# LN1's per-token scale and shift worked out once for eight attention units, the v copies split around the exponential, and a mask moved ahead of a projection

## The reference, cut to what matters

```python
def _layernorm(x, eps=1e-05): return (x - mean(x)) / sqrt(var(x) + eps)
x = x + cross_attention(_layernorm(x), ctx)  # 16 heads of 8, causal mask, softmax, Wo
x = x + ffn(_layernorm(x))                   # 8 experts, top 2 per batch, then a layer norm
```

## Time and profile before

| | us |
|---|---|
| median of 3 runs (lowest, highest) | 616.57 (615.70, 618.05) |
| the profiled execution | 616.13 |
| its span, first to last instruction | 614.2 |
| TensorE matmul busy | 548.9 |
| DVE busy | 524.4 |
| ACT busy | 496.2 |
| POOL busy | 453.7 |

### The profile page before, as it was taken

The page is one execution under the profiler, slowest core; times in us unless marked ns, Lnnn a source line. Parts: engine busy times, 40 slices in busy tenths (PEclk is TensorE's granted clock), DMA queues, the critical chain, the costliest instruction groups (busy, mean ns, idle before and its releaser), DMA issues.

```text
span 614.2 us, 18949 instructions
## 1 busy us (share of the span) xinstructions
PE 548.9 (89%) x4481; PEld 384.0 (63%) x4481; DVE 524.4 (85%) x1473; ACT 496.2 (81%) x1156; POOL 453.7 (74%) x783
## 2 busy tenths in 40 slices
PE   3899999999999999999998617999999999999883
PEld 2556565555555655656555314888788878878672
DVE  3899999999999999999998566888888898898677
ACT  3788888888888888888888627888888888888494
POOL 6789999999999999999997644656555665554355
PEclk9999999999999999999999957999999999999887
DMA  4010101010101000100020011123312331322135
GB/s 121 28 36 11 36 26 34 9 34 26 34 9 34 26 18 25 34 9 15 11 77 2 2 34 56 53 67 91 91 58 62 99 95 56 93 63 65 44 104 171
DMA packets 55568, 30.03 MB, mean 49 GB/s; under 512 B 4840, under 2 KB 54512, under 8 KB 55536
## 3 DMA queue, kind: packets, MB, share of 16 engines
q1 hardware_dynamic: 55104, 29.47, 16.4%
q10 hardware_dynamic: 432, 0.20, 0.1%
HBM read 13.00 MB, written 4.19 MB: 28 GB/s over the span
## 4 chain that ended last, share of the span: by engine, by line
PE 66%; DVE 14%; issue 11%; ACT 5%; DVEq 2%; ACTq 1%; POOL 1%; DMA 0%; POOLq 0%
PE scores_banks L354 9%; PE bank_pair L365 6%; PE scores_banks L484 5%; PE bank_pair L497 5%; PE scores_banks L486 5%; PE scores_banks L485 5%; PE bank_pair L498 5%; PE bank_pair L499 5%; PE bank_pair L378 5%; PE bank L390 5%; ACT v_blocks L540 3%; PE scores_banks L343 3%; DVE scores_shifted L798 2%; PE bank L328 2%; DVE gelu L968 2%
## 5 line engine op out<-in xcount | busy, mean ns | idle before, releaser
L1086 POOL TENSOR_TENSOR probs<-probs,row_sum_recip 128x512 f32<-128x512 f32 x128 | 133.4, 1043 | 20.0 <-DVE row_sum_recip L804 15.0
L693 ACT ACTIVATE gelu<-scores_banks,b_expert 128x512 f32<-128x512 f32 x144 | 98.2, 688 | 26.5 <-PE scores_banks L486 20.5
L1135 POOL CAST gathered<-z_hi_lo (+1 forms) x114 | 45.2, 431 | 88.8 <-PE scores_banks L486 78.8
L788 DVE TENSOR_REDUCE row_max<-scores_banks 128x8 f32<-128x512 f32 x128 | 87.0, 679 | 18.6 <-PE scores_banks L354 18.4
L607 ACT ACTIVATE probsT<-bank_pair 128x512 f32<-128x512 f32 x128 | 76.4, 597 | 27.1 <-PE bank_pair L365 26.2
L596 ACT ACTIVATE probs<-scores_shifted 128x512 f32<-128x512 f32 x128 | 80.0, 625 | 19.3 <-DVE scores_shifted L798 15.7
L917 DVE SCALAR_TENSOR_TENSOR zT_then_yT<-bank_pair,slot_weight,zT_then_yT x288 | 74.3, 282 | 17.3 <-issue 15.6
L791 DVE TENSOR_REDUCE row_sum<-probs 128x8 f32<-128x512 f32 x128 | 86.8, 678 | 1.2 <-ACT probs L596 0.5
L798 DVE TENSOR_TENSOR scores_shifted<-scores_banks,row_max 128x512 f32<-128x512 f32 x128 | 86.6, 677 | 0.0
L354 PE MATMUL scores_banks<-k_by_head,qT 32*64 32x256 f32 x1024 | 84.8, 401 | 0.1
L365 PE MATMUL bank_pair<-ident,probs 128*128 128x128 f32 x512 | 83.9, 286 | 0.3 <-POOL probs L1086 0.2
(11 more groups left out here) (168 smaller groups left out, 1166.2 us busy)
## 6 DMA issues: line engine op xcount, KB each, us to landing
gathered<-z_hi_lo SPq DMA_DIRECT2D x187, 64.0 KB, 1.8
ctxT_pair<-in_ctxT SPq DMA_DIRECT2D x32, 128.0 KB, 2.1
w_raw<-in_w SPq DMA_DIRECT2D x16, 256.0 KB, 3.1
out<-gelu SPq DMA_DIRECT2D x16, 256.0 KB, 2.3
x_res<-in_x SPq DMA_DIRECT2D x14, 256.0 KB, 2.7
x_res<-in_x SPq DMA_DIRECT2D x1, 512.0 KB, 5.3
gathered<-z_hi_lo ACTq DMA_DIRECT2D x3, 64.0 KB, 1.9
wq<-in_wq SPq DMA_DIRECT2D x1, 64.0 KB, 2.5
```

The costliest lines, as they stand in the source:

```text
L693: nc.scalar.activation(G[:, c, :], bank[c][:, :], ACT.Gelu, bias=b1e).then_inc(a_g if c == 0 else a_gp, 1)
L788: nc.vector.reduce_max(mx, ps, AX.X).then_inc(v_max, 1)
L1086: nc.gpsimd.tensor_tensor(pp, pp, RC[:, k % 2, :].unsqueeze(2).to_broadcast([128, 8, S]), ALU.mult).then_inc(g_norm, 1)
```

## The change

The statistics tiles of LN1 hold two groups side by side, and `rstd1` runs once per eight units, in u=4, on four columns (two groups). `stats1` moves on DVE from s=0 (group P+3) to s=2 (group P+4), ahead of `zsum`. In the written-out start the third group's statistics stand in unit 1. The v copies are split: the pair for j2=0 stands ahead of the exp of s=0, the pair for j2=1 behind it. In s=0 TensorE writes the mask of unit u+1 ahead of `project`. Nothing is added or left out in the computation.

```diff
-        MV1 = sb("ln1_mv", [128, 2, 2, 2])
-        RS1 = sb("ln1_rstd", [128, 2])
-        SH1 = sb("ln1_shift", [128, 2])
+        MV1 = sb("ln1_mv", [128, 4, 2])
+        RS1 = sb("ln1_rstd", [128, 4])
+        SH1 = sb("ln1_shift", [128, 4])
...
                         prep_xk(P + 1, (h + 1) % 2)
+                    if s == 0 and (not static or U + 1 < NB):
+                        mask(i, u + 1)
                     if s == 0 and (not static or 0 <= P - 2 < NP):
                         project(4 * i + (2 * h - 3), 1, P - 3, P + 1 if not static else min(P + 1, NP))
...
-                    if not static or U + 1 < NB:
+                    if s > 0 and (not static or U + 1 < NB):
                         mask(i, u + 1)
...
-            def prep_v(P, par):
-                act.wait_ge(p_v, P + 1)
-                ge(act, p_pv, 4 * P - 4)
-                for j2 in range(2):
-                    for odd in range(2):
+            def prep_v(P, par, j2):
+                if j2 == 0:
+                    act.wait_ge(p_v, P + 1)
+                    ge(act, p_pv, 4 * P - 4)
+                for odd in range(2):
...
-            def norm1(P):
-                act.wait_ge(g_sh1, P + 1)
+            def norm1(P, sets, half):
+                act.wait_ge(g_sh1, sets)
...
+                    if s == 0 and (not static or 1 <= P < NP):
+                        prep_v(P, h, 0)
                     if not static or 0 <= U - 1 < NB:
                         act.wait_ge(v_sub, U)
                         ge(act, p_t, U - 4)
                         nc.scalar.activation(PP[:, (u - 1) % 4, :], SS[:, (u - 1) % 2, :], ACT.Exp,
                                              scale=SCALE).then_inc(a_exp, 1)
                     if s == 0 and (not static or 1 <= P < NP):
-                        prep_v(P, h)
+                        prep_v(P, h, 1)
...
-                        norm1(P + 2)
+                        norm1(P + 2, i + 2 + h, 1 - h)
...
-                ge(dve, g_sh1, P - 1)
+                ge(dve, g_sh1, sets)
...
-                    if s == 0 and (not static or P + 3 < NP):
-                        dve.wait_ge(d_x, 16 * i + 16 * h + 16 if not static else max(16 * i + 16 * h + 16, 32))
-                        stats1(P + 3, 1 - h)
+                    if s == 2 and (not static or P + 4 < NP):
+                        dve.wait_ge(d_x, 16 * i + 32)
+                        stats1(P + 4, i + 2 + h, 1 - h)
+                    if static and U == 1:
+                        stats1(3, 2, 0)
+                    if static and P == NP - 4 and s == 2:
+                        dve.nop().then_inc(v_mv1, 2)
                     if s == 2 and (not static or 0 <= P - 3 < NP):
                         zsum(P - 3)
...
-            def rstd1(P, par):
-                pool.wait_ge(v_mv1, 2 * P + 2)
-                ge(pool, a_xn, P)
-                rstd(P, MV1[:, par, :, :], RS1[:, :], SH1[:, :], g_eps1, g_rs1, g_sh1)
+            def rstd1(c, stats, normed, cols=slice(0, 4)):
+                pool.wait_ge(v_mv1, stats)
+                ge(pool, a_xn, normed)
+                rstd(c, MV1[:, cols, :], RS1[:, cols], SH1[:, cols], g_eps1, g_rs1, g_sh1, cols.stop - cols.start)
...
-                    if s == 0 and (not static or P + 2 < NP):
-                        rstd1(P + 2, h)
+                    if u == 4 and (not static or P + 2 < NP):
+                        rstd1(i + 2, 4 * i + 10, 2 * i + 3)
...
-            rstd1(0, 0)
+            rstd1(0, 2, 0, slice(2, 4))
...
-            rstd1(1, 1)
+            rstd1(1, 6, 1)
```

More of the change, by code:

```diff
@@ L533, in _ @@
         def _(act):
-            def prep_v(P, par):
-                act.wait_ge(p_v, P + 1)
-                ge(act, p_pv, 4 * P - 4)
-                for j2 in range(2):
-                    for odd in range(2):
[L540 to L544, removed]
+            def prep_v(P, par, j2):
[3 more added lines that the diff above has]
+                for odd in range(2):
+                    ins = nc.scalar.activation(
+                        VM[64 * j2:64 * j2 + 64, par, :, :, j2, :].rearrange("p (t o) g d -> p o t g d", o=2)[:, odd],
+                        J1[64 * odd:64 * odd + 64, 0:256].rearrange("p (t j g d) -> p j t g d", t=2, j=2, d=HD)[:, j2],
+                        ACT.Copy)
+                    ins.then_inc(a_v if j2 + odd == 2 else a_vh, 1)
             def prep_xk(P):
@@ L564, in norm1 @@
                     nc.scalar.activation(XN[:, k, :], X[:, bass.ds(2 * P + k, 1), :].rearrange("p o d -> p (o d)"),
-                                         ACT.Identity, bias=SH1[:, k:k + 1],
-                                         scale=RS1[:, k:k + 1]).then_inc(a_xnp if k == 0 else a_xn, 1)
+                                         ACT.Identity, bias=SH1[:, 2 * half + k:2 * half + k + 1],
+                                         scale=RS1[:, 2 * half + k:2 * half + k + 1]).then_inc(a_xnp if k == 0 else a_xn, 1)
             def norm2(P):
@@ L628, in _ @@
             nc.scalar.activation(RV[:, 16:17], eps[:, 0:1], ACT.Exp)
-            norm1(0)
+            norm1(0, 1, 1)
             prep_xk(0)
@@ L633, in _ @@
             act.wait_ge(v_setup, 3)
-            prep_v(0, 0)
-            norm1(1)
+            prep_v(0, 0, 0)
+            prep_v(0, 0, 1)
+            norm1(1, 2, 0)
             steps(0)
@@ L729, in link, with stats1 @@
                 dve.wait_ge(v_chain, chain[0])
-            def stats1(P, par):
+            def stats1(P, sets, half):
                 n = 2 * P + 2
@@ L745, in stats1 @@
                 for k in range(2):
-                    nc.vector.bn_aggr(MV1[:, par, k, :], ST1[:, k, :]).then_inc(v_mv1, 1)
+                    nc.vector.bn_aggr(MV1[:, 2 * half + k, :], ST1[:, k, :]).then_inc(v_mv1, 1)
             def residual(T):
@@ L815, in _ @@
             dve.wait_ge(d_x, 16)
-            stats1(0, 0)
+            stats1(0, 0, 1)
             dve.nop().then_inc(v_setup, 1)
@@ L824, in _ @@
             nc.vector.tensor_scalar(WOZ[:, 1, :], WO[:, :], r2mask[:, 1:2], None, ALU.mult).then_inc(v_setup, 1)
-            stats1(1, 1)
+            stats1(1, 0, 0)
             dve.wait_ge(d_x, 32)
-            stats1(2, 0)
+            stats1(2, 1, 1)
             steps(0)
@@ L1029, in causal_mask, with rstd @@
                 pool.nop().then_inc(g_const, 1)
-            def rstd(P, mv, rs, sh, eps_sem, rs_sem, sh_sem):
-                nc.gpsimd.tensor_tensor(rs, mv[:, :, 1], eps[:, 0:2], ALU.add).then_inc(eps_sem, 1)
+            def rstd(P, mv, rs, sh, eps_sem, rs_sem, sh_sem, n=2):
+                nc.gpsimd.tensor_tensor(rs, mv[:, :, 1], eps[:, 0:n], ALU.add).then_inc(eps_sem, 1)
                 nc.gpsimd.tensor_scalar(sh, mv[:, :, 0], -1.0, None, ALU.mult).then_inc(eps_sem, 1)
                 pool.wait_ge(eps_sem, 2 * P + 2)
-                nc.gpsimd.tensor_tensor(rs, rs, minus_half[:, 0:2], ALU.pow).then_inc(rs_sem, 1)
+                nc.gpsimd.tensor_tensor(rs, rs, minus_half[:, 0:n], ALU.pow).then_inc(rs_sem, 1)
                 pool.wait_ge(rs_sem, P + 1)
                 nc.gpsimd.tensor_tensor(sh, sh, rs, ALU.mult).then_inc(sh_sem, 1)
-            def rstd1(P, par):
-                pool.wait_ge(v_mv1, 2 * P + 2)
-                ge(pool, a_xn, P)
-                rstd(P, MV1[:, par, :, :], RS1[:, :], SH1[:, :], g_eps1, g_rs1, g_sh1)
+            def rstd1(c, stats, normed, cols=slice(0, 4)):
+                pool.wait_ge(v_mv1, stats)
+                ge(pool, a_xn, normed)
+                rstd(c, MV1[:, cols, :], RS1[:, cols], SH1[:, cols], g_eps1, g_rs1, g_sh1, cols.stop - cols.start)
             def rstd2(P, h):
```

## The result

The kernel after takes 625.79 us (median of 4 runs, 624.70 to 626.98), the kernel before 616.46 us beside it (4 runs, 615.70 to 618.05): ratio 1.0148, 95% interval 1.0129 to 1.0166. The forecast was 621.0 us in a range of 612.5 to 626.6: slower, as said, but by 9.3 us and not by 4.5. The profiled execution of after took 624.7 us with a span of 623.0, 8.8 over the span before.

What follows compares the result with a forecast made beforehand. Bound by a group's path through TensorE, DVE and ACT, 10.395 us. Split -0.57, mask -0.12, statistics +0.90 give +0.21 per looped group (+5.0); with start +0.9, written-out groups +0.1, end -1.4, about +4.8: 621.0 us, range 612.5 to 626.6.

Steps and rivals of the forecast that it cites:

- The path: Loop group: TensorE (units 1, 2), DVE (unit 2 to subtraction of unit 3), ACT (exp, v copies); 10.35 us summed.
- Their price: LN1's statistics at s=2 on DVE, ahead of z_sums: cost on the path taken as 0.90 us per looped group.
- break-even: Rival: sequencer hides the registers at s=2, statistics' price 0.71 us, +0.02 per group, 616.2 us; chance 0.32.
- t+3.95: DVE's row maximum of unit 2, t being the s=0 projection's start; forecast 4.05 less 0.12 us after t.
- Mask: TensorE, mask pair moved into the stop ahead of the s=0 projection: 0.12 of its 0.22 us gained per group.
- The new stop of the v projection: TensorE waits about 0.6 us for DVE's later residual of s=3 in each looped group.
- the POOL-bound rival: POOL's queue paces the loop; relieving it lets the period fall to 9.9 us, 603 us; chance 0.06.
- the end: From group 28 no statistics, both gains free: period near 9.9 us, -0.45 each for three groups, -1.4 us.
- One sign: Sign of being right: DVE idle 0.4 us or more at the maximum of unit 1.
- exp +0.54: ACT, from start of exp to the v copies behind it: 0.54 us, kept in the sum for the split.
- the start: First wide POOL set waits for third statistics, +0.3 to 0.8; early statistics +0.6; slack returns some: +0.9 us taken.
- the balance of the loop, +0.02: Written-out groups 0 to 3, registers constant: statistics' price 0.71 against both gains, +0.02 us each, +0.1 in all.

Runs made afterwards that it cites:

- e7: The kernel before with only LN1's statistics moved from s=0 to s=2, still for group P+3: 642.51 us, ratio 1.0396.
- e8: The kernel after with all four v copies behind exp again: 639.24 us, ratio 1.0354.
- e1: The kernel after with LN1's statistics back in s=0, for group P+3: 601.9 us, ratio 0.976.
- e10: The kernel before with only the one wide POOL set for eight units: 617.57 us, ratio 1.0008.
- e6: The kernel after with the two v pairs exchanged and the pair ahead of exp in the order odd, even: 622.21 us, ratio 1.0078.
- e3: The kernel before with only the mask moved ahead of the projection in s=0: 614.16 us, ratio 0.996.
- e9: The kernel after with the statistics in s=3, behind the reciprocal, still for group P+4: 611.2 us, ratio 0.9912.
- e2: The kernel before with only the v copies split around exp: 603.95 us, ratio 0.9796.
- e4: The kernel after with the two v pairs exchanged (j2=1 ahead of exp, j2=0 behind): 626.27 us, ratio 1.015.
- e12: The kernel before with split v copies, early mask, three repeated start masks, v pairs exchanged and first pair odd, even: 604.89 us, ratio 0.9809.

## Why the prediction was right or wrong

**Right, by its own steps.** The path, with statistics in s=2 on it: e7 (+25 us), e8 (+22), e1 (-24 against after). Their price: 0.83 and 0.89 us in the two kinds of group, mean 0.86, taken as 0.90 (over the 0.84 that parted it from break-even). The maximum at t+3.95, forecast 3.93. Mask 0.095 us, taken as 0.12. The new stop of the v projection for the residual, in each of the 25 groups, with 0.4 or 0.5 us of TensorE's own idle time, forecast 0.6. POOL off the path (e10), so the POOL-bound rival falls, and with it, for this kernel, the ranking by occupancy of the Trainium skill ("Perfetto Trace Analysis", section Identifying the Most-Contended Engine), by which POOL, level with DVE, was worth relieving. The period at the end: the maxima of unit s=1 at 325.47 and 335.32, 9.85 us, forecast 9.9. One sign missed: DVE was to idle 0.4 us or more at the maximum of unit 1, and it idles 0.28, with 0.15 more ahead of the residual in front of it.

**Wrong: the term "exp +0.54" behind the split.** The sum carried the 0.54 us of the earlier trace rows over, from exp to a first copy that reads a bank from partition 0, into a place where the last reader of a bank had started at partition 64. There it is 0.66. This is +0.12 us per group, 2.9 of the missing 3.5 us of the loop; e6, which brings 0.54 back, is 3.2 us shorter over the 24 groups. A term of the sum was mis-sized; the mechanism held: ACT ends the group, not TensorE, by 0.15 to 0.2 us as the distance from mask to projection shows, where 0.1 was forecast. The rest of the 0.15 us per group between 0.21 and 0.36: z_sums behind the statistics lasts 0.42 us instead of 0.37, and the next instruction follows at 0.33 instead of 0.28, +0.05; the mask gives 0.095 and not 0.12, +0.025; the statistics give 0.04 back.

**Wrong: the start.** Forecast +1.0 to unit 16, measured +2.4. The forecast gave group 1 the balance of the loop, +0.02, and let later slack take some back. Instead units 6 and 7 come 0.49 and 0.59 us later: the maximum of unit 6 waits 0.76 us for its scores (0.38 in before), so what DVE had won by the statistics gone from unit 4 is mostly lost again, and unit 7 stands behind the group's own statistics. The split can't help there, since the first projection of an s=0 comes in group 2. Unit 1 is 0.74 us late, inside the 0.3 to 0.8 of the forecast: POOL waits 0.22 us for the third statistics, its power on four columns takes 1.04 us instead of 0.72, and the scores of unit 1 take 0.89 us instead of 0.66, because TensorE's clock was lower. Stretches view of after, 16 to 20 us (the granted clock is the third number from the right):

```profile
16.00:18.00 2.00, 2.00 (x14) 0.97 (x13) 0.49 (x1) 0.60 (x1) 0.87 (x2) 0.70 0.00 0
18.00:20.00 2.00, 2.00 (x13) 0.56 (x12) 1.90 (x7) 0.57 (x2) 0.73 (x2) 0.50 0.00 0
```

0.50 is the level of 1.2 GHz; TensorE had idled 1.88 us before 15.51, in before 1.35 us. The slow matmuls are not the change's own, though: they stood at the start of most profiles (e1, e3 to e9), in e3 after 1.16 us idle, and not behind that stretch in before, e2 or e10. In e3 the same scores took 1.13 us with a granted clock of 1.00 shown, so that column doesn't account for all of them, and their cause stays open. The statistics in units 1 and 2 cost 0.75 and 0.63 us, with 0.82 back up to unit 5: +0.56, forecast 0.6, right but for what unit 6 lost of it.

**Wrong, to the other side: the end.** Counted as three groups of 0.45 us; there are four, since the last statistics stand in group 27, and each gives 0.5 to 0.6. -2.16 us instead of -1.4.

Together: 1.4 (start) + 3.5 (loop, against 5.0 and the 0.2 for the stop) - 0.8 (end) is the 4.1 us between the forecast of +4.8 and the measured +8.9 at the last maximum.

## What to carry to other kernels

Work moved from an engine's free stretch into its critical stretch costs its whole price, here 24 us for 0.86 us per group, however many instructions the move saves on an engine that nobody waits for: look at what stands next behind the new place, and whether it waits for something anyway. A duration from start to start belongs to a pair of neighbours and to what they read before; when a change gives an instruction a new neighbour, bound the term by the same instruction behind another kind. And a written-out start or end is a case of its own: ask there again which terms are on the path.

## What was not expected of the hardware

**ACT's spacing depends on the partitions at which neighbours start.** Exp to the next copy takes 0.54 us or 0.65 to 0.66, z_hi_lo to the first pair 0.30 or 0.44, first pair to exp 0.47 or 0.59. The longer ones are the length of what stands ahead (0.63, 0.42, 0.56) and 0.02 or 0.03 us more, as if ACT started only when it had ended. Each longer one stands where the instruction reads a bank from another start partition than the last one that read a bank (the second pair in after and e4, the first in e12), or writes to another than the last one wrote (exp in e12, behind copies that write from 64). The Trainium skill ("VectorE: DVE Perf Modes", section Two Vector instructions with no wait between them) states such a rule for Vector instructions, kept apart by memory; by it, applied to ACT, all of these cases come out as measured. The reading condition is shown alone, by e4 against e6. The writing condition rests on exp in e12, where the order of the copies ahead changed with it, so it is inferred.

**POOL's power** takes 0.71 to 0.73 us on two columns and 1.02 to 1.04 on four, the other three instructions of the set the same on both within 0.01 us. The Trainium skill's figure per element ("GPSIMD Engine Reference", section 3.1), measured there on an addition, would have made the wider power free; the trace disagrees for the power, by 0.15 us a column, and agrees for the addition.

**The same four statistics instructions** take 0.71 to 1.09 us from the first start to the next instruction, by their place: in s=0 0.71, or 0.99 behind the loop's branch; in s=2 0.83 or 0.89; in s=3 0.72, or 1.09 with the branch behind them.
